# Scatters of gathered rows with at most two under way, in a fused attention and mixture-of-experts kernel

## The chip, the cores and the metric

The kernel runs on 1 core of one Trainium2 chip, as one program with one launch. The metric is the device time of an execution in microseconds (us); the median of several executions is compared. Lower is better.

## What is computed

Two layers on x of 8 batches x 512 tokens x 256 channels. The first is cross-attention with 16 heads of 16 channels, the second a mixture of 8 experts of which each token uses 2.

```python
x = x + xattn(layernorm(x), ctx)      # 16 heads, softmax(q k^T / 4) v, then wo
t = layernorm(x)
probs = softmax((t @ Wg + bg) / 5.0)
vals, idx = top_k(probs, 2)
gates = mask(vals, idx) / (sum + 1e-9)
h = gelu(t @ W1[e] + b1[e])           # hidden size 512, each expert e
y = sum_e gates[e] * (h @ W2[e] + b2[e])
x = x + y
```

Everything is float32; products are made of two or three float32r products where they must be exact.

## The kernel before, in words

The program is written by hand for each engine, with semaphores, and there is no scheduler. Each engine runs its own list in order.

**Attention.** Eight bodies, one for each batch (`body(i)` on every engine), each of four units of four heads. A unit has eight steps of 1.7 to 2 us. In a step TensorE makes two score products (L1542 for the maximum that VectorE takes at L1113, L1555 for the exponentials that ScalarE takes at L1041) and the products with the values (L1568). Between the steps stand the small units of work of earlier and later batches, which the tables `PREP`, `POST`, `LATE` and `LAST_POST` place at a group and step: "OP0" to "OP3" (the output projection, L1619, taken by VectorE at L1166), "V0" and "V1" (the values of the next batch, L1609), "MT" (the transposed maxima, L1577), "XG0" and "XG1" (the transposes of the normalised rows `xg`, L1586), "LG" (the gate logits, L1629) and "PX" (positions of the chosen rows).

**Routing and scatters.** For each batch b, `ln2(b)` on POOL (L791 to L807) writes the normalised rows into `xg` (128 partitions x 4 tiles x 265 floats: 256 channels, 8 gates, the token's number). VectorE adds the gates and computes in `route_rows` which row of `xs_dram` (the experts' regions in device memory) each token's copy goes to. POOL's `scatter_tile(k, t)` (L813) then sends one tile of 128 rows with an indirect DMA: 8 of them for a batch, for choice k = 0, 1 and tile t = 0 to 3. Each adds 16 to the one semaphore `scattered` when it has landed. There are 64 in all:

- batches 0 to 4 in bodies 2 to 6 (`scatter(i - 2, ...)`, L818), each held back until step 5 and later steps of unit 1 by a wait on `st_full`;
- batch 5 in body 7, without that pacing;
- batch 6 in the tail, one before each of the tiles 1 to 8, and batch 7 before each of the tiles 25 to 32 (L930 to L937).

`ln2(b + 1)` follows the eight scatters of the batch on POOL and waits at L796 until all of them have landed, since it writes `xg` again. Behind it on POOL stand `add_bo`, `place_v` (L871, which waits for TensorE's L1568 of the body) and `low_staged` (L830). SP waits for `xg_done` in `load_w2` (L572), and in body 7 for the scatters of batches 0 to 5 before its first `load_rows`. VectorE waits for those of batches 0 to 6 in `apply_last`.

**Tail.** 71 tiles of 128 rows: SP loads a tile from `xs_dram` (L625), TensorE makes hidden and output products (L1716, L1734), VectorE scales the result into `y_sb` (L1467), and POOL's `add_out(j)` (L922) adds it into `out` with an indirect DMA, after reading from a table for how many earlier ones it has to wait. POOL's list is `add_out` and, between them, the scatters.

All DMAs of POOL go through one queue (q0 in the profile), those of SP through another (q1).

Of the kernel before, what the change touches and what calls it, by code (L numbers as in the profile page):

```python
# [14 lines left out]
P = 128  # L15
B, S, D = 8, 512, 256
H, DH = 16, 16
NT = S // P
# [185 lines left out]
def build(nc, x, ctx_kv, wqT, bq, wkT, bk, wvT, bv, woT, bo, wg, bg, w1, b1, w2, b2, out):  # L204
    with ExitStack() as stack:
# [185 lines left out]
        kv_in, qk_weights_in = sem("kv_in"), sem("qk_weights_in")  # L391
        ones_set, ident_set, bq_scaled = sem("ones_set"), sem("ident_set"), sem("bq_scaled")
        warm_set = sem("warm_set")
# [26 lines left out]
        chosen_done, rows_done, token_chain = sem("chosen_done"), sem("rows_done"), sem("token_chain")  # L420
        scattered, padded = sem("scattered"), sem("padded")
        pad_rows_done, tab_done = sem("pad_rows_done"), sem("tab_done")
# [31 lines left out]
        def w2_hi_free(eng, e):  # L454

            if e < 2:
                eng.wait_ge(st_full, NP * G)
            elif e < 6:
                eng.wait_ge(pv_done, NT * (G - 1) + (2 if e < 4 else 1))
            else:  # L460
                eng.wait_ge(st_full, NP * (G - 1))

        def stage_no(i, n):
# [6 lines left out]
        def _(sp):  # L470
# [156 lines left out]
            def body(i):  # L627
# [54 lines left out]
                if not more:  # L682
                    sp.wait_ge(tab_done, 1)
                    sp.wait_ge(scattered, 16 * TOPK * NT * EARLY_B)
                    for j in range(EARLY_XS + 1):
                        load_rows(j)
# [58 lines left out]
            for j in range(AHEAD, TILES):  # L745
                if j == TAIL_STORE:
                    store_out(B - 1)
                if j == TAIL_PAD:
                    pad_regions()
                if j == TILES1:  # L750
                    sp.wait_ge(tab_done, 2)
                    sp.wait_ge(scattered, 16 * TOPK * NT * B)
                    sp.wait_ge(padded, 16 * (E + 1))
                load_rows(j)
# [3 lines left out]
        def _(pool):  # L758
            nc.gpsimd.memset(ident[:], 0.0).then_inc(pool_chain, 1)
            pool.wait_ge(pool_chain, 1)  # L760
            nc.gpsimd.affine_select(out=ident[:], in_=ident[:], compare_op=ALU.not_equal, fill=1.0, base=0,
                                    pattern=[[-1, P]], channel_multiplier=1).then_inc(ident_set, 1)
            nc.gpsimd.memset(mhalf[:], -0.5).then_inc(pool_chain, 1)
            nc.gpsimd.memset(oT[0:2, 0, :], 1.0).then_inc(ones_set, 1)
            nc.gpsimd.memset(pad[:], 0.0).then_inc(ones_set, 1)
            for g in range(NG):
                nc.gpsimd.memset(kq[g][:, 1].bitcast(F32), 0.0).then_inc(ones_set, 1)
            pool.wait_ge(pool_chain, 2)
            pool.wait_ge(stats_done, 1)
            nc.gpsimd.tensor_tensor(rstd[:], veps[:], mhalf[:], ALU.pow).then_inc(rstd_done, 1)  # L770
            nc.gpsimd.memset(v_aug[:], 0.0).then_inc(pool_chain, 1)
            pool.wait_ge(pool_chain, 3)
            nc.gpsimd.memset(v_aug[:, :, :, DH:DH + 1], 1.0).then_inc(pool_chain, 1)
            pool.wait_ge(pool_chain, 4)
            nc.gpsimd.memset(before[:], 1.0).then_inc(pool_const, 1)
# [15 lines left out]
            def ln2(b):  # L791
                pool.wait_ge(ln2_stats, b + 1)
                nc.gpsimd.tensor_tensor(rstd2[:], veps2[:], mhalf[:], ALU.pow).then_inc(rstd2_done, 1)
                if b > 0:
                    pool.wait_ge(scattered, 16 * TOPK * NT * b)
                    pool.wait_ge(full["XG1"], b)  # L796
                    pool.wait_ge(token_chain, 2 * b)
                else:
                    pool.wait_ge(pool_const, 11)
# [13 lines left out]

            def scatter_tile(k, t):
                pool.indirect_dma_start(out=xs_dram, out_offset=bass.IndirectOffsetOnAxis(ap=rows[:, k, t:t + 1], axis=0),  # L815
                                        in_=xg[:, t, :], in_offset=None).then_inc(scattered, 16)

            def scatter(b, paced=None):  # L818
                rows_ready(b)
                for k in range(TOPK):  # L820
                    for t in range(NT):
                        if paced is not None:

                            pool.wait_ge(st_full, paced + NT * k + t)
                        scatter_tile(k, t)

# [100 lines left out]
            for j in range(TILES):  # L927
                if j == TAIL_POW:
                    ln2(B - 1)
                if j == TAIL_SCATTER_BEFORE:  # L930
                    rows_ready(B - 2)
                if TAIL_SCATTER_BEFORE <= j < TAIL_SCATTER_BEFORE + TOPK * NT:
                    scatter_tile(*divmod(j - TAIL_SCATTER_BEFORE, NT))
                if j == TAIL_SCATTER:
                    rows_ready(B - 1)
                if TAIL_SCATTER <= j < TAIL_SCATTER + TOPK * NT:
                    scatter_tile(*divmod(j - TAIL_SCATTER, NT))  # L937
                if j == TILES1:
                    pool.wait_ge(out_done, 16 * B)
                    pool.wait_ge(need_done, 2)  # L940
                add_out(j)
# [164 lines left out]
        def _(dve):  # L1106
# [82 lines left out]
            def apply_last(b, half):  # L1189
                dve.wait_ge(rstd2_done, b + 1)  # L1190
                dve.wait_ge(full["XG1"], b)
                dve.wait_ge(scattered, 16 * TOPK * NT * b)
                for t in (2 * half, 2 * half + 1):
# [318 lines left out]
        def _(pe):  # L1512
# [155 lines left out]
            for n in range(WARM):  # L1668
                nc.tensor.matmul(ring[2][:, 1, :], xgT[:, 0, 0:P], xgT[:, 0, :], start=True, stop=True)
            pe.wait_ge(ident_set, 1)  # L1670
            for name in PROLOGUE:
# [125 lines left out]
```

## Time and profile before

| | us |
|---|---|
| median of 3 executions | 808.66 |
| their range | 805.75 to 810.44 |
| profiled execution, its own time | 804.46 |
| profiled execution, its span | 802.4 |
| TensorE busy in the span | 755.2 |
| VectorE busy | 612.2 |
| ScalarE busy | 455.1 |
| POOL busy | 393.9 |
| mean granted TensorE clock | 0.992 |

The span is the time between the first and the last instruction of the profile; the execution's own time holds 2.06 us around it. Times in the rows are from the span's start. "Idle before" in brackets is how long the engine stood still before the instruction and what released it; "issue" is time in which it waited for nothing that the profile shows, "remote" a release that the profile can't name. TensorE's ends are modelled.

### The profile page before, as it was taken

The page shows a single profiled execution, that of the slowest core. Times are in us where ns is not written, and L with a number is a line of the kernel's source. Part 1 is how long each engine was busy: PE and PEld are TensorE (multiplying, and loading weights), DVE is VectorE, ACT ScalarE, POOL GpSimd, SP SyncE. Part 2 cuts the span into 40 slices and gives each one's busy share as a digit, 9 for nine tenths or more (in the row PEclk, how much of TensorE's full clock was granted, in tenths as well). Part 3 has the DMA queues.
Part 4 walks back from the last instruction along what each step waited for, and adds up shares of the span by engine and source line. Part 5 has one row for each costly group of instructions (what it writes and reads, how often), then busy time and mean ns, then how long its engine had stood idle before and what let it go on. Part 6 is the DMA issues. An engine that isn't in the chain of part 4 may idle for free.

```text
span 802.4 us, 16337 instructions
## 1 busy us (share of the span) xinstructions
PE 755.2 (94%) x4672; PEld 451.9 (56%) x4672; DVE 612.2 (76%) x1126; ACT 455.1 (57%) x663; POOL 393.9 (49%) x357
## 2 busy tenths in 40 slices
PE   9999999999999999999999898869999999999994
PEld 4443344444444444444444333349989888999994
DVE  6787778798697787788788787667777887776773
ACT  2066676776766766766676674854345443444441
POOL 6506143547637728728725613306553564444443
PEclk9999999999999999999999999999999999999998
DMA  7665857657666767757658467666454465454441
GB/s 226 208 179 176 228 165 226 209 179 250 206 188 239 213 198 234 190 188 250 186 174 268 149 178 260 257 241 161 89 101 80 79 145 93 74 84 70 72 69 12
DMA packets 90660, 136.24 MB, mean 170 GB/s; under 512 B 15456, under 2 KB 49216, under 8 KB 90192
## 3 DMA queue, kind: packets, MB, share of 16 engines
q1 hardware_dynamic: 76592, 117.33, 48.0%
q0 software_dynamic: 13296, 17.09, 12.1%
q8 instruction: 43, 0.70, 0.4%
q10 hardware_dynamic: 688, 0.79, 0.3%
q14 instruction: 41, 0.34, 0.1%
HBM read 71.25 MB, written 64.04 MB: 169 GB/s over the span
## 4 chain that ended last, share of the span: by engine, by line
PE 71%; DMA 7%; DVE 7%; ACT 6%; issue 5%; SPq 2%; POOL 1%; POOLq 0%; DVEq 0%; another core or an unknown queue 0%
PE ps_pv L1568 13%; PE ring L1555 10%; PE ring L1734 9%; PE ring L1716 8%; PE ring L1542 7%; PE ps_x L1599 7%; ACT probs L1041 4%; PE ps_x L1619 4%; DMA out<-y_sb,xs 3%; PE ps_x L1609 3%; PE ring L1725 3%; DVE negm L1113 2%; PE ps_x L1629 2%; DMA den<-oT 2%; PE ps_pv L1707 1%
## 5 line engine op out<-in xcount | busy, mean ns | idle before, releaser
L1113 DVE TENSOR_REDUCE negm<-ring 128x2 f32<-128x1024 f32 x256 | 310.2, 1222 | 73.0 <-PE ring L1542 65.0
L1041 ACT ACTIVATE probs<-ring 128x1024 f32<-128x1024 f32 x256 | 260.0, 1024 | 91.7 <-PE ring L1555 79.4
L922 POOL DMA_INDIRECT out<-y_sb,xs x71 | 110.2, 1553 | 152.3 <-DMA out<-y_sb,xs 73.6
L1568 PE MATMUL ps_pv<-probs,v_aug 128*32 128x512 f32 x1024 | 136.8, 606 | 4.0 <-ACT probs L1041 3.9
L1555 PE MATMUL ring<-kq 64*128 64x512 f32 x512 | 125.4, 491 | 7.5 <-DVE negm L1113 7.3
L1542 PE MATMUL ring<-kq 64*128 64x512 f32 x512 | 105.9, 412 | 10.6 <-ACT probs L1041 5.4
L1555 PEld LDWEIGHTS ring<-kq 64*128 64x128 f32 x512 | 47.4, 183 | 108.5 <-issue 72.4
L1074 ACT CAST xsT_hi<-ps_pv 128x256 fp32r<-128x256 f32 x70 | 26.1, 373 | 133.8 <-PE ps_pv L1707 122.9
L1734 PE MATMUL ring<-w_hi,hT_hi 128*128 x284 | 85.3, 300 | 0.1
L815 POOL DMA_INDIRECT xs_dram<-xg,rows x64 | 63.3, 988 | 39.9 <-issue 15.9
L1734 PE MATMUL ring<-w_lo,hT_hi 128*128 x284 | 80.0, 282 | 0.0
L1734 PE MATMUL ring<-w_hi,hT_lo 128*128 x284 | 79.5, 280 | 0.0
L1455 DVE TENSOR_TENSOR h_pre<-ring,b_sb 128x512 f32<-128x512 f32 x71 | 48.9, 690 | 20.8 <-PE ring L1716 19.0
L1542 PEld LDWEIGHTS ring<-kq 64*128 64x128 f32 x512 | 48.7, 186 | 26.7 <-issue 10.8
L1716 PE MATMUL ring<-w_hi,xsT_hi 128*128 x142 | 58.8, 414 | 4.4 <-DVE xsT_lo L1443 3.2
L855 POOL CAST qk_hi<-qk 128x512 fp32r<-128x512 f32 x28 | 17.1, 611 | 86.0 <-ACT qk L977 54.3
L871 POOL TENSOR_TENSOR v_aug<-v_flat,bv_sb 128x256 f32<-128x256 f32 x32 | 23.7, 756 | 71.0 <-PE ps_pv L1568 61.0
L1716 PE MATMUL ring<-w_hi,xsT_lo 128*128 x142 | 56.4, 397 | 0.0
L1716 PE MATMUL ring<-w_lo,xsT_hi 128*128 x142 | 56.2, 396 | 0.0
L1734 PEld LDWEIGHTS ring<-w_hi,hT_hi 128*128 128x128 f32 x284 | 53.6, 189 | 0.2 <-issue 0.2
L1734 PEld LDWEIGHTS ring<-w_lo,hT_hi 128*128 128x128 f32 x284 | 53.6, 189 | 0.0
L1734 PEld LDWEIGHTS ring<-w_hi,hT_lo 128*128 128x128 f32 x284 | 53.5, 188 | 0.0
(197 smaller groups left out, 1223.4 us busy)
## 6 DMA issues: line engine op xcount, KB each, us to landing
kq<-k_dram SPq DMA_DIRECT2D x64, 192.0 KB
kq<-q_dram SPq DMA_DIRECT2D x64, 192.0 KB
xs<-xs_dram SPq DMA_DIRECT2D x71, 132.5 KB
k_dram<-qk_hi SPq DMA_DIRECT2D x32, 256.0 KB
q_dram<-qk_hi SPq DMA_DIRECT2D x32, 256.0 KB, 2.8
o_dram<-oT SPq DMA_DIRECT2D x32, 256.0 KB
w_dram<-w_sb SPq DMA_DIRECT2D x12, 512.0 KB
w_hi<-w_dram SPq DMA_DIRECT2D x12, 512.0 KB, 7.4
```

The lines of the kernel that those rows point to most:

```text
L815: pool.indirect_dma_start(out=xs_dram, out_offset=bass.IndirectOffsetOnAxis(ap=rows[:, k, t:t + 1], axis=0), in_=xg[:, t, :], in_offset=No ...
L922: pool.indirect_dma_start(out=out, out_offset=bass.IndirectOffsetOnAxis(ap=xs[j % AHEAD][:, TOKEN:TOKEN + 1].bitcast(I32), axis=0), in_=y_ ...
L1041: nc.scalar.activation(probs[kt][:, 2 * jp:2 * jp + 2, :], ring[PLACE["ST", u, p] % RINGS][:], ACT.Exp).then_inc(exp_done, 1)
L1113: nc.vector.tensor_reduce(negm[:, v % 2, :, jp, kt], ring[PLACE["MX", v, p] % RINGS][:], AX.X, ALU.max, negate=True).then_inc(max_free, 1)
L1455: v.tensor_tensor(h_pre[:, j % 2, :], ps_h[j % 2], b1_sb[:, bass.ds(e, 1), :].rearrange("p o h -> p (o h)"), ALU.add).then_inc(f_h_out, 1)
L1542: mm = nc.tensor.matmul(ps[:, h, :], kq[g][lo:lo + HALF, 1, jp, kt * P:(kt + 1) * P], kq[g][lo:lo + HALF, 0, jp, :], start=True, stop=True)
L1555: mm = nc.tensor.matmul(ps[:, h, :], kq[g][lo:lo + HALF, 0, jp, kt * P:(kt + 1) * P], kq[g][lo:lo + HALF, 1, jp, :], start=True, stop=True)
L1568: mm = nc.tensor.matmul(ps_pv[2 * DH * j:2 * DH * (j + 1), :], v_aug[:, kt, HPG * g + j, :], probs[kt][:, j, :], start=(kt == 0), stop=(kt ...
L1599: mm = nc.tensor.matmul(ps[:, half], w[:, c, f * P:(f + 1) * P], act_t[:, c, half], start=(c == 0), stop=(c == DC - 1))
L1619: mm = nc.tensor.matmul(ps[:, (t % 2) * D:(t % 2 + 1) * D], numT[:, c, t * P:(t + 1) * P], wo_sb[:, c, :], start=(c == 0), stop=(c == DC - 1))
L1716: mm = nc.tensor.matmul(ps_h[j % 2], x[:, j % 2, c, :], w[:, bass.ds(e, 1), c, :].rearrange("p o h -> p (o h)"), start=(n == 0), stop=(n = ...
L1734: mm = nc.tensor.matmul(ps_y[j % 2][:, 0:D], h[:, j % 2, c, :], w[:, bass.ds(e, 1), c, :].rearrange("p o d -> p (o d)"), start=(n == 0), s ...
```

## The change

`scattered` becomes two semaphores, used in turn by the number n of the scatter (0 to 63). From the third on, a scatter waits on POOL until all scatters of its own semaphore before it have landed: scatter n waits for scatter n - 2. Whoever waited for the first b batches now waits for both semaphores. To make room for the second one, `ident_set` goes away: the identity's `affine_select` counts in `pool_chain`, whose later thresholds go up by one, and TensorE waits there for 2. No instruction moves to another place on any engine.

```diff
-        ones_set, ident_set, bq_scaled = sem("ones_set"), sem("ident_set"), sem("bq_scaled")
+        ones_set, bq_scaled = sem("ones_set"), sem("bq_scaled")
...
-        scattered, padded = sem("scattered"), sem("padded")
+        scattered, padded = [sem(f"scattered{n}") for n in range(2)], sem("padded")
...
+        def wait_scattered(eng, b):
+
+            for n in range(2):
+                eng.wait_ge(scattered[n], 16 * TOPK * NT * b // 2)
...
-                    sp.wait_ge(scattered, 16 * TOPK * NT * EARLY_B)
+                    wait_scattered(sp, EARLY_B)
...
-                    sp.wait_ge(scattered, 16 * TOPK * NT * B)
+                    wait_scattered(sp, B)
...
-                                    pattern=[[-1, P]], channel_multiplier=1).then_inc(ident_set, 1)
+                                    pattern=[[-1, P]], channel_multiplier=1).then_inc(pool_chain, 1)
...
-            pool.wait_ge(pool_chain, 2)
+            pool.wait_ge(pool_chain, 3)
...
-                    pool.wait_ge(scattered, 16 * TOPK * NT * b)
+                    wait_scattered(pool, b)
...
-            def scatter_tile(k, t):
+            def scatter_tile(b, k, t):
+
+                n = NT * (TOPK * b + k) + t
+                if n >= 2:
+                    pool.wait_ge(scattered[n % 2], 16 * (n // 2))
                 pool.indirect_dma_start(out=xs_dram, out_offset=bass.IndirectOffsetOnAxis(ap=rows[:, k, t:t + 1], axis=0),
-                                        in_=xg[:, t, :], in_offset=None).then_inc(scattered, 16)
+                                        in_=xg[:, t, :], in_offset=None).then_inc(scattered[n % 2], 16)
...
-                    scatter_tile(*divmod(j - TAIL_SCATTER_BEFORE, NT))
+                    scatter_tile(B - 2, *divmod(j - TAIL_SCATTER_BEFORE, NT))
...
-                    scatter_tile(*divmod(j - TAIL_SCATTER, NT))
+                    scatter_tile(B - 1, *divmod(j - TAIL_SCATTER, NT))
...
-                dve.wait_ge(scattered, 16 * TOPK * NT * b)
+                wait_scattered(dve, b)
...
-            pe.wait_ge(ident_set, 1)
+
+            pe.wait_ge(pool_chain, 2)
```

## Rows read from the trace of the kernel before

**Rows 1.** The page: busy time by engine, and the chain that ended last
```profile
PE 755.2 (94%) x4672; PEld 451.9 (56%) x4672; DVE 612.2 (76%) x1126; ACT 455.1 (57%) x663; POOL 393.9 (49%) x357
...
PE 71%; DMA 7%; DVE 7%; ACT 6%; issue 5%; SPq 2%; POOL 1%; POOLq 0%; DVEq 0%; another core or an unknown queue 0%
```

**Rows 2.** POOL's instructions in order, batch 0's scatters: start, length, [idle before]
```profile
189.04 1.27 POOL L815 DMA_INDIRECT xs_dram<-xg,rows  x1 [0.19 <-issue]
...
190.61 0.97 POOL L815 DMA_INDIRECT xs_dram<-xg,rows  x1 [0.30 <-issue]
...
195.67 0.96 POOL L815 DMA_INDIRECT xs_dram<-xg,rows  x1 [0.30 <-issue]
...
199.31 0.96 POOL L815 DMA_INDIRECT xs_dram<-xg,rows  x1 [0.30 <-issue]
...
203.89 0.20 POOL L800 CAST xg<-token 128x4 int32<-128x4 f32 x1 [1.40 <-DMA xs_dram<-xg,rows]
```

**Rows 3.** The same view, the last scatter of batch 1 and its follower
```profile
261.42 0.96 POOL L815 DMA_INDIRECT xs_dram<-xg,rows  x1 [0.30 <-issue]
...
267.29 0.19 POOL L800 CAST xg<-token 128x4 int32<-128x4 f32 x1 [2.09 <-DMA xs_dram<-xg,rows]
```

**Rows 4.** Stretches 190 to 202 us: busy times, granted clock, DMA share, GB/s
```profile
193.00:196.00 3.00, 3.00 (x19) 1.28 (x13) 3.00 (x4) 2.35 (x4) 2.25 (x3) 1.00 0.30 103
...
196.00:199.00 3.00, 2.06 (x16) 0.54 (x14) 1.58 (x4) 1.20 (x2) 1.58 (x2) 1.00 0.95 256
```

**Rows 5.** POOL after the batch of body 2, and SP's queue in that body
```profile
224.41 0.74 POOL L871 TENSOR_TENSOR v_aug<-v_flat,bv_sb 128x256 f32<-128x256 f32 x1 [7.58 <-PE ps_pv L1568]
...
215.99 0.40 SPq L572 DMA_DIRECT2D x_all<-in_L_ffn_W  x1
...
225.15 0.54 SPq L513 DMA_DIRECT2D kq<-mT  x1
```

**Rows 6.** POOL in body 7: the batch without pacing and ln2 behind it
```profile
487.77 1.11 POOL L815 DMA_INDIRECT xs_dram<-xg,rows  x1 [14.49 <-DVEq L1281]
...
496.79 0.96 POOL L815 DMA_INDIRECT xs_dram<-xg,rows  x1 [0.30 <-issue]
...
505.59 1.04 POOL L793 TENSOR_TENSOR rstd<-veps,mhalf 128x4 f32<-128x4 f32 x1 [7.85 <-DVE veps L1187]
...
506.80 4.95 POOL L804 TENSOR_SCALAR xg<-x_all,mv,rstd 128x256 f32<-128x256 f32 x4
```

**Rows 7.** TensorE in body 7: the transposes of xg
```profile
512.13 0.66 PE L1586 MATMUL ps_x<-ident,xg 128*128 128x128 f32 x4
```

**Rows 8.** Stretches of body 7, columns as in rows 4
```profile
487.00:495.00 8.00, 6.64 (x33) 2.68 (x33) 6.67 (x8) 3.48 (x4) 5.70 (x6) 0.79 1.00 356
...
501.00:504.00 3.00, 2.56 (x18) 1.35 (x18) 3.00 (x5) 1.37 (x2) 0.00 (x0) 1.00 0.00 0
```

**Rows 9.** POOL in the tail: a scatter and the last but one before it
```profile
565.19 0.98 POOL L815 DMA_INDIRECT xs_dram<-xg,rows  x1 [0.31 <-issue]
...
571.51 0.98 POOL L815 DMA_INDIRECT xs_dram<-xg,rows  x1 [0.30 <-issue]
```

**Rows 10.** The chain that ended last, in order of time: start, us, what
```profile
573.12 5.72 DMA out<-y_sb,xs
...
792.31 2.70 DMA out<-y_sb,xs
```

**Rows 11.** TensorE: MT and V0 in body 1, then in body 2
```profile
133.06 0.28 PE L1577 MATMUL ps_x<-ident,negm 128*16 128x128 f32 x1
...
137.37 0.92 PE L1609 MATMUL ps_x<-wv_sb,kvT 128*128 128x256 f32 x3
...
193.80 0.28 PE L1577 MATMUL ps_x<-ident,negm 128*16 128x128 f32 x1
...
199.31 0.92 PE L1609 MATMUL ps_x<-wv_sb,kvT 128*128 128x256 f32 x3
```

**Rows 12.** VectorE in body 7, just after the sixth scatter
```profile
497.83 0.42 DVE L1166 TENSOR_TENSOR x_all<-x_all,ps_x 128x256 f32<-128x256 f32 x1 [2.46 <-remote]
```

More of the change, by code:

```diff
@@ L771, in _ @@
             nc.gpsimd.memset(v_aug[:], 0.0).then_inc(pool_chain, 1)
-            pool.wait_ge(pool_chain, 3)
+            pool.wait_ge(pool_chain, 4)
             nc.gpsimd.memset(v_aug[:, :, :, DH:DH + 1], 1.0).then_inc(pool_chain, 1)
-            pool.wait_ge(pool_chain, 4)
+            pool.wait_ge(pool_chain, 5)
             nc.gpsimd.memset(before[:], 1.0).then_inc(pool_const, 1)
@@ L824, in scatter @@
                             pool.wait_ge(st_full, paced + NT * k + t)
-                        scatter_tile(k, t)
+                        scatter_tile(b, k, t)
             def low_staged(i, n):
```

## The prediction

> **What bounds the kernel now.** I read the page first: TensorE is busy for 755.2 us of 802.4 (94%), and the chain that ended last is TensorE's for 71%, while POOL has 1% of it [rows 1]. So work on POOL costs time only where somebody waits for it. The scatters are 64 POOL instructions of about 1 us, and the question is how long one needs to land, for which of the 64 the new wait is not met yet, and who stands behind POOL then.
>
> POOL's own list shows the first batch [rows 2]. Its first scatter starts at 189.04, the second at 190.61, the sixth at 195.67, the eighth at 199.31: a first step of 1.57 us, then 1.265 us each ((195.67 - 190.61) / 4), a little more at the last two, which the pacing holds. The follower at L800 waits for the landing and starts at 203.89, that is 4.58 us after the eighth scatter began. In batch 1 the same distance is 267.29 - 261.42 = 5.87 us [rows 3]. I call this distance L: from the start of a scatter to the start of an instruction that waits for its landing. Both are taken where SP's transfers crowd in: the share of the DMA engines is 0.95 in 196 to 199 us. Three microseconds before it is only 0.30, at 103 GB/s [rows 4]; one scatter moves 128 x 265 x 4 = 135,680 bytes, which at 1.265 us each is 107 GB/s. So the scatters land as fast as they are issued there, and nothing piles up. For a quiet queue the nearest row is the add_out near the end: 2.70 us from its start to its landing [rows 10].
>
> **The change part by part.** With the new wait scatter n can't start before n - 2 has landed. Two can be under way, so a batch of eight becomes four pairs: if L is the same for all, the last has landed 1.57 + 4 L after the first began. The wait binds where L is over twice the step, 2.53 us.
>
> *L, from both sides.* It can't be under the 0.96 us in which POOL itself works on the instruction [rows 2]; the highest row is 5.87. I take 2.70 for scatters that meet an idle queue (nearest row, add_out) and 5.87 for those that meet a full one. By the Trainium skill, page "DMA: Bandwidth & Descriptors", section "Anatomy of one DMA — SWDGE (gpsimd) path", a DMA from this queue costs about 2.0 us plus its bytes at 436 GB/s, most of it the receipt of the write; an estimate by it is 2.31 us, with the 0.96 before it 3.27, and by it the batch in body 7 would have landed after 14.7 us and delay nobody. The rows say up to 5.87, and by that a batch takes 25.05 us; I reckon with the rows.
>
> *Bodies 2 to 6* (40 scatters). Now the follower of a batch starts 14.85 us after its first scatter (203.89 - 189.04). With L = 2.70 the last scatter could start after 3 x 2.70 + 1.57 = 9.67 us, and it starts at 10.27 already now, so nothing moves. With 5.87 throughout the follower comes 10.2 us later. What covers it: POOL stands idle for 7.58 us before its L871 at 224.41, waiting for TensorE [rows 5]; SP issues the load at L572, which waits for xg, at 215.99, and its next urgent one, the maxima of L513, at 225.15 [rows 5]. ln2 now ends at about 209 us (203.89 + 0.20 + 4.84 for the four tiles, the same length as in body 7 [rows 6]), 7 us before SP's turn; even 10.2 us late it would hold SP for 3.2 us, inside the stretch before 225.15. Expected delay 0 to 1 us on POOL, on the end 0. Both ends are 0 as well.
>
> *Body 7* (8 scatters). This is the tight place. The scatters begin at 487.77 without pacing. ln2 starts at 505.59, held by VectorE's statistics and not by them, and its next instruction, which does wait for them, can start at 506.63. It then makes xg until 511.75 (506.80 + 4.95) [rows 6], and TensorE takes its transposes at 512.13 [rows 7], with only 0.38 us between. So the scatters may take 506.63 - 487.77 = 18.86 us, and the point from which they delay TensorE is L = (18.86 - 1.57) / 4 = 4.32 us. In 487 to 495 us the DMA engines are full (share 1.00), in 501 to 504 they stand idle (0.00) [rows 8]. I take 5.87 for the first pair and 2.70 for the three others: 1.57 + 5.87 + 3 x 2.70 = 15.54 us, landed at 503.3, 3.3 us early. Cost 0; the ends are 0 and, with 5.87 for all, 25.05 - 18.86 = 6.2 us. SP's wait for the six batches stands later still and needs nothing earlier.
>
> *Tail* (16 scatters). Here a scatter and the last but one are at least one add_out and a tile apart, as 565.19 and 571.51, 6.32 us [rows 9]. The longest landing that the chain shows there is an add_out's of 5.72 us [rows 10], the scatters' own highest is 5.87. So the wait is met, by 0.45 us at the worst. This matters, since POOL is on the chain in this stretch. Value 0.
>
> *The waits themselves.* Scatters in bodies 2 to 6 carry a wait (`st_full`), those in the tail carry none, and both start 0.30 us after the instruction before [rows 2, 9]. A wait that is met costs nothing visible. I take 0; the upper end is another 0.30 us for each of the about six tail scatters that stand where POOL is on the chain, 1.8 us. In the bodies 8 x 0.30 us would vanish in the 7.58 us of idle time.
>
> *The identity's semaphore.* POOL's list keeps its order, count 2 of `pool_chain` is reached by the same instruction as before, and the memset that counts 3 ran before the same wait. Cost 0.
>
> **Sum.** 804.46 (the profiled execution, span 802.4) + 0 = 804.5. The median of the three is 4.2 us above that execution, so for the median the sum is 808.66 + 0, and I say 808.8 for the few waits that may show. A change of 0.5% (4.04 us) is about what a measurement of this kernel can tell from none; the three executions differ by 4.7 us.
>
> **The rivals.**
>
> *Faster: a standstill that comes with the bursts.* From MT to V0 TensorE needs 137.37 - 133.06 = 4.31 us in body 1, which has no scatters, and 199.31 - 193.80 = 5.51 in body 2 [rows 11], with the same work. The 1.20 us fall just behind the sixth scatter (195.67). In body 7, where neither the step nor SP's list is the same, VectorE stands for 2.46 us before 497.83 with no named release [rows 12], again behind the sixth scatter. If this comes from transfers that pile up, fewer under way could end it: 5 x 1.20 + 2.46 = 8.5 us, 800.3. Against it: in body 2 the step and the traffic before the standstill say that no more than about two are under way already (DMA share 0.30), so the wait hardly changes the moment at which it comes. By the Trainium skill, the same page, section "Queues, rings and completion order", each DMA engine takes turns between the queues by packets, so that a shorter POOL queue would leave SP's transfers more turns. By that rule the trace agrees in so far as the standstill of body 2 comes where both queues are in use [rows 4]. The rival's chance is 0.16.
>
> *Slower: body 7's batch lands late.* If L stays at 5.87 for all four pairs (SP's loads in front [rows 8]), ln2 waits, xg comes 6.2 us late, TensorE stands at XG0 and with it everything to the tail: 815.0. It decides from L = 4.32 on; at 4.58 it is 1.0 us. For it: 4.58 and 5.87 are what POOL really waited elsewhere. Against it: the queues are empty after 501 us. Chance 0.11 for over half of it.
>
> *The change does nothing at all.* With L under 2.53 no wait ever binds. That is 808.7, not to be told from the forecast by time, only by POOL's rows; it is counted with it.
>
> **How the numbers follow.** Forecast, with the case of no binding wait, 0.73: 808.8, own range 805.5 to 812 by the scatter of the executions. Faster rival 0.16 (800.3, in part 804), slower rival 0.11 (815.0, in part 812). The range takes in most of the faster case and half of the slower: 801.0 to 813.5. Faster by over 0.5%: 0.17. Slower by over 0.5%: 0.12. Within: 0.71.
>
> **What would show it.** Right: in bodies 2 to 6 POOL's scatters still start 1.3 to 1.6 us apart for the first six, with short waits for a landing at most at the last two, ln2 within 1 us of where it was; in body 7 a wait of 3 to 5 us before the third scatter, all eight landed before 506; no wait for a scatter in the tail; MT to V0 still 5.5 us in body 2. Wrong: POOL waiting for landings at every pair, XG0 in body 7 later than 512 by more than a microsecond with ln2 as its releaser, waits for landings before scatters in the tail (then add_out and VectorE's L1467 are late behind them), or MT to V0 back at 4.3 us.

## The result: 1.5% slower, and the profile after

The changed kernel takes 820.3 us (median of 6 executions, 814.49 to 824.88), the kernel before beside it 809.82 (805.75 to 810.84): ratio 1.0154, 95% interval 1.0116 to 1.0192. The forecast of no difference was wrong, and 820.3 lies outside the range of 801.0 to 813.5. The profiled execution took 816.67 us, with a span of 814.6 us; before it was 804.46 and 802.4.

The page of the changed kernel: busy time by engine (to read beside [rows 1]), and the group of all scatters (line, engine, what | busy, mean ns | idle before, by releaser).
```profile
PE 759.5 (93%) x4672; PEld 452.1 (56%) x4672; DVE 611.1 (75%) x1126; ACT 456.4 (56%) x663; POOL 393.7 (48%) x357
...
L824 POOL DMA_INDIRECT xs_dram<-xg,rows x64 | 63.0, 985 | 73.7 <-DMA xs_dram<-xg,rows 29.3
```
TensorE is busy for 4.3 us more with the same 4672 instructions, which points to its clock (mean granted 0.981, before 0.992); the rest of the 12.2 us of span is idle time. POOL now waits 29.3 us for landings in front of scatters. Who pays for them is not POOL.

POOL in the changed kernel, batch 0 and what follows it (start, length, what, [idle before <-releaser]), which answers to [rows 2]:
```profile
189.06 1.27 POOL L824 DMA_INDIRECT xs_dram<-xg,rows  x1 [0.19 <-issue]
190.63 0.97 POOL L824 DMA_INDIRECT xs_dram<-xg,rows  x1 [0.30 <-issue]
193.68 0.96 POOL L824 DMA_INDIRECT xs_dram<-xg,rows  x1 [2.08 <-DMA xs_dram<-xg,rows]
...
196.91 0.96 POOL L824 DMA_INDIRECT xs_dram<-xg,rows  x1 [1.01 <-DMA xs_dram<-xg,rows]
199.91 0.96 POOL L824 DMA_INDIRECT xs_dram<-xg,rows  x1 [2.03 <-DMA xs_dram<-xg,rows]
202.56 0.96 POOL L824 DMA_INDIRECT xs_dram<-xg,rows  x1 [1.70 <-PE ring L1564]
204.88 0.96 POOL L824 DMA_INDIRECT xs_dram<-xg,rows  x1 [1.36 <-PE ring L1564]
205.86 1.06 POOL L798 TENSOR_TENSOR rstd<-veps,mhalf 128x4 f32<-128x4 f32 x1
211.89 0.20 POOL L805 CAST xg<-token 128x4 int32<-128x4 f32 x1 [4.97 <-issue]
```
The third scatter starts 4.62 us after the first, the last 15.8 us after it where it was 10.3. Its follower at L805 comes another 7.01 us later, at 211.89 instead of 203.89: ln2 is 8.0 us late.

SP in that moment: its load of the next expert's w1 (512 KB), the largest transfer near the last scatter. Two of 256 KB go out just before it, at 203.44 and 204.42.
```profile
205.06 0.45 SPq L480 DMA_DIRECT2D w_sb<-in_L_ffn_W  x1
```

TensorE in the kernel before, body 2: MT, XG0 and the next MT. (MT comes four times in a body. "Unit 1" is from here on the stretch from the MT of [rows 11], at 193.80 in body 2, to the next at 210.27, and "unit 2" the one behind it, with XG0 in it.)
```profile
210.27 0.28 PE L1577 MATMUL ps_x<-ident,negm 128*16 128x128 f32 x1
...
214.19 0.66 PE L1586 MATMUL ps_x<-ident,xg 128*128 128x128 f32 x4
...
224.13 0.28 PE L1577 MATMUL ps_x<-ident,negm 128*16 128x128 f32 x1
```
The same of the changed kernel, and XG0 of bodies 3 to 6:
```profile
209.10 0.28 PE L1586 MATMUL ps_x<-ident,negm 128*16 128x128 f32 x1
...
217.05 1.08 PE L1595 MATMUL ps_x<-ident,xg 128*128 128x128 f32 x4 [3.96 <-POOL xg L809]
...
229.24 0.28 PE L1586 MATMUL ps_x<-ident,negm 128*16 128x128 f32 x1
...
284.47 0.84 PE L1595 MATMUL ps_x<-ident,xg 128*128 128x128 f32 x4 [3.71 <-POOL xg L809]
...
349.35 0.88 PE L1595 MATMUL ps_x<-ident,xg 128*128 128x128 f32 x4 [2.90 <-POOL xg L809]
...
412.81 0.63 PE L1595 MATMUL ps_x<-ident,xg 128*128 128x128 f32 x4 [1.44 <-POOL xg L809]
...
474.36 0.63 PE L1595 MATMUL ps_x<-ident,xg 128*128 128x128 f32 x4 [1.25 <-POOL xg L809]
```
Before, xg was ready at 204.07 + 4.84 = 208.9 (L804 starts right behind the follower) and read at 214.19: TensorE's margin was 5.3 us (4.0 to 5.5 in the other four bodies), and a delay of 8.0 us breaks it. That alone makes a wait of 2.7 us; TensorE also comes 1.2 us earlier than before (its MT is at 209.10, not 210.27), and so waits 3.9. Over the five bodies it waits 3.96, 3.71, 2.90, 1.44 and 1.25 us, 13.3 in all, and unit 2 grows from 13.86 to 20.14 us in body 2, over the five bodies from 69.1 to 86.8: 17.7 us. The other 4.4 stand in bodies 2 to 4, where the granted clock is 0.50 for 6.8, 3.4 and 3.4 us from about the end of the wait on. Windows of the changed kernel (us, PE, PEld, DVE, ACT, POOL busy, granted clock, DMA share, GB/s):
```profile
216.00:223.00 7.00, 5.95 (x24) 2.63 (x24) 1.23 (x1) 2.23 (x4) 7.00 (x7) 0.53 0.92 314
```
and of the kernel before:
```profile
216.00:223.00 7.00, 6.89 (x52) 3.71 (x44) 5.40 (x6) 4.27 (x5) 0.83 (x1) 1.00 1.00 334
```
Half a microsecond before the end of the wait of 3.96 us the granted clock falls to its lower level, 1.2 GHz, and stays there for 6.8 us, and 24 matmuls start where 52 did.

Something was won as well. MT and V0 of body 2, changed kernel, beside [rows 11]:
```profile
193.83 0.28 PE L1586 MATMUL ps_x<-ident,negm 128*16 128x128 f32 x1
...
198.13 1.99 PE L1618 MATMUL ps_x<-wv_sb,kvT 128*128 128x256 f32 x8
```
4.30 us, not 5.51: the standstill behind the sixth scatter is gone. Unit 1 takes 15.27 or 15.28 us in every body, where it took 16.45 to 16.88: 6.8 us less over five bodies. The first scatter of body 7 thus starts 17.7 - 6.8 + 0.8 (the other units) = 11.7 us late, at 499.43.

Body 7 in the changed kernel, POOL, to read beside [rows 6]:
```profile
499.43 1.11 POOL L824 DMA_INDIRECT xs_dram<-xg,rows  x1 [14.49 <-DVEq L1290]
...
506.57 0.96 POOL L824 DMA_INDIRECT xs_dram<-xg,rows  x1 [4.75 <-DMA xs_dram<-xg,rows]
...
515.18 0.96 POOL L824 DMA_INDIRECT xs_dram<-xg,rows  x1 [0.70 <-DMA xs_dram<-xg,rows]
...
520.30 0.19 POOL L805 CAST xg<-token 128x4 int32<-128x4 f32 x1 [2.92 <-issue]
```
and TensorE, its MT and XG0, beside [rows 7]:
```profile
513.79 0.28 PE L1586 MATMUL ps_x<-ident,negm 128*16 128x128 f32 x1
...
525.48 1.08 PE L1595 MATMUL ps_x<-ident,xg 128*128 128x128 f32 x4 [4.20 <-POOL xg L809]
```
Eight scatters and the follower take 20.87 us against the 18.86 that I had allowed, and TensorE waits 4.20 us. The stretch before it is 2.6 us shorter (16.51 us from MT to MT, before 19.08), so the first add_out is 13.7 us late and the last 12.1. The tail between them is 1.6 us shorter than before (252.6 us for 254.2). In the twenty profiled executions of this document the tail lasts 251.8 to 258.8 us, so nothing is read from that difference.

POOL in the tail of the changed kernel:
```profile
578.45 0.98 POOL L824 DMA_INDIRECT xs_dram<-xg,rows  x1 [0.30 <-issue]
...
584.76 0.98 POOL L824 DMA_INDIRECT xs_dram<-xg,rows  x1 [0.30 <-issue]
```
No wait for a landing there, and 0.30 us before each of the 16 as in [rows 9].

### The profile page after: what moved, and what is told of

The parts are those of the page before. It is cut to its first block and busy times, and to the rows that moved or that the text cites. A ratio compares the mean times of both kernels' runs of the same rounds, so it can differ in the third digit from the quotient of the medians.

```text
span 814.6 us, 16384 instructions
## 1 busy us (share of the span) xinstructions
PE 759.5 (93%) x4672; PEld 452.1 (56%) x4672; DVE 611.1 (75%) x1126; ACT 456.4 (56%) x663; POOL 393.7 (48%) x357
## 3 DMA queue, kind: packets, MB, share of 16 engines
q0 software_dynamic: 13296, 17.09, 12.1%
## 5 line engine op out<-in xcount | busy, mean ns | idle before, releaser
L1577 PE MATMUL ps_pv<-probs,v_aug 128*32 128x512 f32 x1024 | 140.7, 622 | 3.0 <-ACT probs L1050 2.7
L824 POOL DMA_INDIRECT xs_dram<-xg,rows x64 | 63.0, 985 | 73.7 <-DMA xs_dram<-xg,rows 29.3
L1457 DVE TENSOR_TENSOR hT_lo<-ring,hT_hi 128x512 fp32r<-128x512 f32 x71 | 48.8, 688 | 4.7 <-ACT hT_hi L1089 1.1
```

The costliest lines, as they stand in the source:

```text
L1457: v.tensor_tensor(hT_lo[:, j % 2], ps_ht[j % 2].rearrange("p (c t) -> p c t", t=P), hT_hi[:, j % 2].bitcast(F32), ALU.subtract).then_inc(f ...
L1577: mm = nc.tensor.matmul(ps_pv[2 * DH * j:2 * DH * (j + 1), :], v_aug[:, kt, HPG * g + j, :], probs[kt][:, j, :], start=(kt == 0), stop=(kt ...
```

## The experiments

They ran in five sessions, each beside executions of the kernel before on the same chip; its median was 805.9 and 806.0 us in the first two and 795.7, 795.5 and 798.0 in the others. That difference became a finding; across sessions only ratios are compared. The chip had number 12, 5, 0, 0 and 5, so under number 5 the kernel before took 806.0 us once and 798.0 another time.

### Which waits cost: none, bodies 2 to 6, body 7, the tail

These are the changed kernel, with the wait in `scatter_tile` under another condition. Shown is the one for body 7; for bodies 2 to 6 it is `2 <= n < 40`, for the tail `n >= 48`. The first kernel has no wait at all, only the two semaphores.
```
-                if n >= 2:
+                if 40 <= n < 48:
                     pool.wait_ge(scattered[n % 2], 16 * (n // 2))
```


> The change without its waits before the scatters: two semaphores in turn, nobody held back. Theory A (the time is lost because the batch's last scatter lands late, ln2 waits for it, and TensorE stands at XG0): as the kernel before, 809.8 us, no wait at XG0, and MT to V0 again 5.5 us in body 2. Theory B (each wait costs by itself, or the bookkeeping of two semaphores): over 812 us even so.

> Waits only before the scatters of bodies 2 to 6 (38 of the 62). Theory A: these bodies lose 17.7 us at XG0 (waits of 1.3 to 4.0 us and a slower clock behind them) and win back 6.7 us at the standstill, so about 820.5 us. Theory B, waits of equal price: 38/62 of the loss of 10.5 us, 816 us.

> Waits only before the eight scatters of body 7. Theory A: 2.6 us won at the standstill and about 4 lost at XG0, 811 us. Theory B: 8/62 of 10.5 us, 811 us. The trace tells: under A the standstill before 497.8 is gone and XG0 comes late.

> Waits only before the 16 scatters of the tail. Theory A: met at once, 809.8 us. Theory B: 16/62 of 10.5 us, 812.5 us, or more, since POOL is on the chain there.

Measured: no waits 805.73 us, ratio 0.9985 (0.9955 to 1.0014); bodies 2 to 6 811.51, 1.0070 (1.0036 to 1.0103); body 7 806.70, 1.0006 (0.9981 to 1.0030); tail 805.99, 1.0005 (0.9971 to 1.0039). So the two semaphores, the identity's count and the tail's waits show no cost, as forecast, and bodies 2 to 6 cost. But they cost about half of what theory A forecast (820.5 beside 809.8, a ratio of 1.013), and the 1.0070 is what the rival of equal prices gave (816, 1.008): these four times alone don't decide between the two. That rival falls later, with kernels that keep many waits and lose nothing by them.

The profiled execution with the waits of bodies 2 to 6 has the changed kernel's picture: unit 1 at 15.27 us, unit 2 at 19.87, 18.30, 19.75, 14.76 and 14.39. It took 819.95 us, 8.4 more than its kernel's median, so it shows where the time goes, and not how much a typical execution loses. In body 7 alone the slow side and the fast side cancel. TensorE there, and the window behind its XG0 (columns as above):
```profile
501.16 0.28 PE L1586 MATMUL ps_x<-ident,negm 128*16 128x128 f32 x1
...
510.27 0.87 PE L1595 MATMUL ps_x<-ident,xg 128*128 128x128 f32 x4 [1.62 <-POOL xg L809]
```
```profile
510.00:524.00 14.00, 13.73 (x60) 6.87 (x60) 4.94 (x16) 8.00 (x11) 0.33 (x2) 0.52 0.87 321
```
The stretch to this MT shrank from 19.08 to 16.51 us, and XG0 waits 1.62 us, with the clock at 0.52 in 510 to 524. (With no waits in body 7 that stretch varies among these four kernels: 17.66 us with no waits at all, 17.73 with those of bodies 2 to 6, 19.73 with those of the tail.) The batch and its follower took 18.25 us, less than the 18.86 that I had allowed; TensorE waits all the same, because without the standstill it comes sooner. The parts sum to about 0.8%, the whole was 1.5% in its session: when body 7's batch follows late bodies, XG0 waits 4.20 us instead of 1.62. That is at most a part of the gap, and the rest stays open.

### Is it TensorE's margin at XG0? The transposes later, with a control

The transposes move two steps back, and the two halves of the gate logits become one piece of work.
```
-        (3, 3): "XG0", (3, 4): "XG1", (3, 5): "LG0", (3, 7): "LG1"}
+        (3, 5): "XG0", (3, 6): "XG1", (3, 7): "LG"}
```


> The change, and XG0, XG1 and LG of bodies 2 to 6 two steps (about 3.5 us) later, at steps 5, 6 and 7 of the last unit. Theory A (TensorE waits at XG0 for the late batch, and its clock falls behind that wait): waits of 4.0, 3.7, 2.9, 1.4 and 1.3 us shrink to 0.5 us at most, the clock stays up, the 6.7 us won at the standstill remain, so 14 us less than the change, about 806 in its scale of 820 and at or below the kernel before. Theory B (waits cost wherever they stand): within 2 us of the change.

> The kernel before with XG0, XG1 and LG of bodies 2 to 6 two steps later and nothing else: the control of e1. Both theories: as before within 1 us, since TensorE does the same work and nothing waits for LG early.

Measured: the changed kernel with it 812.83 us, 1.0080 (1.0043 to 1.0116); the kernel before with it 813.58, 1.0090 (1.0055 to 1.0126). The move itself costs 0.9%, where none was expected, so it is no remedy, but beside this control the change costs nothing, with all its 62 waits in place. XG0 of body 2, with the waits and the late transposes:
```profile
222.07 0.66 PE L1595 MATMUL ps_x<-ident,xg 128*128 128x128 f32 x4
```
No wait, although the last scatter starts at 210.65; of bodies 3 to 6 one has a wait, of 0.29 us. So with the waits at XG0 of these bodies gone, the loss is gone too, or the main part of it: the 6 us of standstills should then have shown as a gain, and didn't. Body 7, which the move leaves as it was, still waits 2.42 us; unit 2 took 2.5 us more in sum than in the control, and one other unit grew to 18.08 us, with 6.8 us at half clock at its start.

### Keeping the gain without the loss: fewer waits, or a pace

First the changed kernel without waits for the last two scatters of a batch, then the kernel before with a later pace (each scatter of bodies 2 to 6 is held by a softmax tile two steps later) and no wait for a landing.
```
-                if n >= 2:
+                if n >= 2 and n % 8 < 6:
```
```
-SCATTER = 5
+SCATTER = 7
```


> The change without the waits before the last two scatters of each batch. Theory A: those two start up to 2.5 us earlier and ln2 comes 2 to 3 us earlier in bodies 2 to 6, so XG0 waits 1 us or less in place of up to 4: 8 to 10 us less than the change. The standstill stays away. Theory B: 16 of 62 waits fewer, 3 us less.

> The kernel before with one semaphore and no wait for a landing, but the pacing of the scatters two steps later (SCATTER 7): from the fifth on one scatter for each step, some 1.8 us apart where it was 1.27. Theory C1 (the standstill behind the sixth scatter comes from six in a row at 1.27 us): the first MT interval of bodies 2 to 6 falls from 16.5 to 15.3 us, the last scatter is 3 us later and ln2 within the 5 us that XG0 leaves: 6 us faster. Theory C2 (it comes from the number of scatters, however spaced): 16.5 us stays, time as before.

Measured: first six 800.09 us, 0.9923 (0.9888 to 0.9959); paced 801.74, 0.9951 (0.9915 to 0.9987). Both beat the kernel before, in a session where it took 805.98 and the control above, with the same scatters, still has unit 1 at 16.22 to 16.77 us. In both unit 1 is 15.27 us and unit 2 13.87 (13.67 in body 6). The first of them keeps 46 of the 62 waits. The last scatter of batch 0 and its follower, first six:
```profile
202.46 0.96 POOL L824 DMA_INDIRECT xs_dram<-xg,rows  x1 [0.30 <-issue]
...
205.46 0.20 POOL L805 CAST xg<-token 128x4 int32<-128x4 f32 x1 [0.94 <-DMA xs_dram<-xg,rows]
```
and paced:
```profile
202.53 0.96 POOL L815 DMA_INDIRECT xs_dram<-xg,rows  x1 [0.71 <-PE ring L1555]
...
205.66 0.20 POOL L800 CAST xg<-token 128x4 int32<-128x4 f32 x1 [1.09 <-DMA xs_dram<-xg,rows]
```
They start 3.2 us later than in the kernel before, and the follower only 1.6 to 1.8 us later, inside TensorE's 5.3. Two waits fewer move the last scatter by 2.4 us, and the follower by 6.4. In body 7 the first of them still waits, 2.42 us at XG0.

### Three under way, and one pause only

```
-        scattered, padded = [sem(f"scattered{n}") for n in range(2)], sem("padded")
+        scattered, padded = [sem(f"scattered{n}") for n in range(3)], sem("padded")
...
-                if n >= 2:
-                    pool.wait_ge(scattered[n % 2], 16 * (n // 2))
+                if n >= 3:
+                    pool.wait_ge(scattered[n % 3], 16 * (n // 3))
```
and, in another kernel, `if n % 8 in (2, 3):` in the place of `if n >= 2:`.

> The changed kernel with three semaphores in turn instead of two: each scatter waits for the last but two. Theory (margin and standstill): the change lost its time because the last scatter of a batch started 5.6 us later (204.88 for 199.31), past the 5.3 us by which TensorE reads xg late at XG0, and won back about 1.3 us a body because the standstill behind six scatters in a row went. With three under way only the sixth, the seventh and the eighth wait at all, by one to two us: last scatter of batch 0 at 200.5 to 202.5, rows of batch 1's ln2 copied (L805) at 204 to 206, no wait of TensorE at XG0, unit 2 of a body 13.9 us. If the standstill hangs on how many scatters are under way, unit 1 is 15.3 us and the time 799 to 803; if it hangs only on six issues at 1.27 us one behind the other, it is gone too where the sixth is held. Rival (any wait for a landing costs TensorE its clock, whatever the margin): half clock in the bodies as in the changed kernel and a time of 810 or more.

> The changed kernel with the wait only before the third and fourth scatter of a batch, so that one pause of about 1.8 us is left and the other six scatters follow at 1.27 us (the seventh and eighth by the work's own pace). Theory: last scatter of batch 0 at 200 to 201, ln2's copy at 204, unit 2 of a body 13.9 us, no wait at XG0. The standstill: if it needs six scatters at 1.27 us in an unbroken row, the row is now third to eighth, and either it comes behind the eighth or, with the pace of the seventh, it is gone; if it hangs on the bytes that stand in the queue, it comes back behind the sixth (unit 1 16.5 us). Time 799 to 803 without it, 804 to 807 with it. Rival (each wait for a landing costs by itself): half of the changed kernel's loss, 810 to 813.

Measured: 798.3 us, 1.0013 (0.9993 to 1.0033), and 797.8, 1.0014 (0.9991 to 1.0036). In microseconds both are about a microsecond below the 799 to 803 that were expected, with unit 1 at 15.27, unit 2 at 13.86, and no wait at XG0 in bodies 2 to 6, so the rivals that any wait for a landing costs, or each the same, are out. But the kernel before took 795.74 us beside them: there was nothing to win. In body 7 of the first, TensorE stands for 1.04 us and then, at XG0, for 0.92; behind that its granted clock is at 0.51 for 14 us, though it is busy all the time (columns as above):
```profile
506.00:520.00 14.00, 14.00 (x60) 6.92 (x60) 5.10 (x17) 8.18 (x11) 0.02 (x1) 0.51 0.80 293
```
The question about the standstill was not answered by them; it was asked again below.

### The slow landing: SP's w1 load a step later

```
-                if i < B - 2:
+                if i == 0:
                     load_w1(i)
-                if i == 0:
                     load_w1(E - 2)
                 if more:
                     put_max(i + 1, 0)
                     load_stack(i + 1, 2)
+                    if 0 < i < B - 2:
+                        load_w1(i)
```


> The changed kernel, but SP's load of the next expert's w1 in bodies 1 to 5 (L480, at 205.06 in body 2, 0.2 us behind the last scatter's start) is issued one step later, behind the next V's keys and queries (about 212). Theory (the last scatter is slow because it stands behind this load): from its start to ln2's copy falls from 7.0, 6.4, 5.8 and 5.6 us in bodies 2 to 5 to 4.0 to 4.4, body 6, which has no such load, stays at 4.3; TensorE's wait at XG0 falls by the same 1.4 to 2.7 us; time 3 to 8 us below the changed kernel. Rival (the load is innocent, the landing is slow for another reason, such as the stores and fetches before it): 5.6 to 7.0 us as before and no change of the time.

> The control of the run before: the same later w1 load in the kernel before the change. There the last scatter starts 5.7 us ahead of that load and lands ahead of it, so both theories expect no difference beyond 0.3% (804 to 808 us); a gain or a loss here is what moving the load does by itself, and is to be taken off the other run's.

Measured: the changed kernel with it 805.76 us, 1.0118 (1.0070 to 1.0167); the kernel before with it 797.09, 1.0005 (0.9979 to 1.0031). From the last scatter's start to the follower it now takes 3.99, 4.60, 4.72 and 4.89 us in bodies 2 to 5, not 7.01, 6.44, 5.77 and 5.59. The waits at XG0 of bodies 2 to 6 are 0.94, 1.60, 0.57, 1.81 and 1.23 us, 6.2 in all instead of 13.3, though the one in body 5 is longer than the 1.44 it had. The forecast of 4.0 to 4.4 was a little short. And the control showed unit 1 at 15.27 us in the kernel before, with none of its edits near the scatters.

### Is the standstill always there? Four kernels in one session

The kernel before, the changed kernel, the latter with the late w1 load, and the paced kernel, each unchanged from above.

> The kernel before, unchanged, to have its trace on the same chip as the next three. Theory (the standstill belongs to the chip's own speed at taking packets, not to the kernel alone): where unit 1 of a body lasts 16.4 to 16.9 us the time is about 806, where it lasts 15.3 us it is about 797. Rival (the standstill went in the last four runs through their edits): unit 1 lasts 16.4 us or more in every body of this run, whatever its time.

> The changed kernel, on the same chip. Waits of TensorE at XG0 in bodies 2 to 6 of 1.2 to 4.0 us, unit 2 of a body 15 to 20 us, unit 1 15.3 us. Theory: the loss against the kernel before is the growth of unit 2 (about 17 us) and of body 7 (about 3) less what the standstills took: 1.2 to 1.8 per cent where the kernel before has them, 2.0 to 2.8 per cent where it has not. Rival (the gain never came from the standstill): the same 1.5 per cent on every chip.

> The changed kernel with SP's w1 load of bodies 1 to 5 behind the next V's keys and queries, on the same chip as the changed kernel. Theory: the last scatter's start to ln2's copy is 4.0 us instead of 5.6 to 7.0, TensorE's wait at XG0 is 1 to 2.5 us shorter, and the time is 6 to 11 us below the changed kernel's: about half of the loss was this load. Rival (the loss is the waits alone, the landing does not matter): the time is that of the changed kernel within 3 us.

> The kernel before with its scatters paced by the softmax's tiles two steps later, no wait for a landing. Theory: where the kernel before has the standstill this is 0.5 to 1.2 per cent faster (unit 1 at 15.3 us), where it has not it is the same within 0.3 per cent. Rival (pacing gains by something else): 0.5 per cent faster or more on either.

Measured, beside 795.46 us: the kernel before under its own label 797.09, 1.0027 (1.0010 to 1.0045); changed 814.10, 1.0258 (1.0185 to 1.0330); with the late load 807.55, 1.0140 (1.0104 to 1.0175); paced 795.77, 0.9997 (0.9973 to 1.0022). The first of these, the same kernel twice, shows that 0.3% can come from nothing.

The kernel before beside them, the seventh and eighth scatter on POOL, and TensorE's MT, V0 and MT:
```profile
197.37 0.96 POOL L815 DMA_INDIRECT xs_dram<-xg,rows  x1 [0.30 <-issue]
198.65 0.96 POOL L815 DMA_INDIRECT xs_dram<-xg,rows  x1 [0.32 <-PE ring L1555]
```
```profile
194.23 0.28 PE L1577 MATMUL ps_x<-ident,negm 128*16 128x128 f32 x1
...
198.53 1.99 PE L1609 MATMUL ps_x<-wv_sb,kvT 128*128 128x256 f32 x8
...
209.50 0.28 PE L1577 MATMUL ps_x<-ident,negm 128*16 128x128 f32 x1
```
MT to V0 is 4.30 us and unit 1 15.27 with eight scatters in an unbroken row of 1.27 us: no standstill, in any body. The rival, that it was the edits, is out. (The seventh scatter stood 2.38 us behind the sixth in the first trace, and stands 1.27 behind it here: what held it there was the standstill, by way of the softmax tile that it waits for.) Without a standstill the change has nothing to gain, and costs 2.6% instead of 1.5; the paced kernel gains nothing either, as expected. How the 2.6% come about is not shown by the profiled execution. Unit 2 sums to 75.9 us there, 6.9 more than in the kernel before beside it and not the 17 expected; the first add_out is 9.2 us late, and 4.9 us more fall in the tail, where no wait stands. In four profiled executions with the waits of bodies 2 to 6, unit 2 takes 17.7, 17.9, 6.9 and (further below) 11.2 us more than the 69.1 of the kernel before. The late load took 6.5 us from the changed kernel's time. Its profiled execution didn't say why, with waits at XG0 of about the same sum, so both ran again.

> The changed kernel again. Theory: in bodies where SP's w1 load is issued within half a microsecond of the last scatter's start, ln2's copy comes 5.8 to 7 us after that start and TensorE waits 3 to 4 us at XG0, behind which its granted clock is at 1.2 GHz for some microseconds; where the load comes over 1.2 us later, 4.2 to 5.6 us and waits under 1.5 us.

> The changed kernel with the w1 load of bodies 1 to 5 a step later, again. Theory: from the last scatter's start to the copy 4.0 to 5.4 us in every body, no wait at XG0 above 2.2 us, the time 4 to 9 us below the changed kernel's. Rival (the gain is elsewhere, or chance): the sum of the five waits at XG0 is within 2 us of the changed kernel's, and the time too.

Measured, beside 797.98 us: changed 813.48, 1.0199 (1.0158 to 1.0239); late load 807.24, 1.0126 (1.0088 to 1.0164). Again about 6 us apart. Body 5 of the changed kernel, first SP's load:
```profile
394.64 0.45 SPq L480 DMA_DIRECT2D w_sb<-in_L_ffn_W  x1
```
then POOL's last scatter and its follower:
```profile
394.41 0.96 POOL L824 DMA_INDIRECT xs_dram<-xg,rows  x1 [1.44 <-DMA xs_dram<-xg,rows]
...
400.68 0.19 POOL L805 CAST xg<-token 128x4 int32<-128x4 f32 x1 [4.23 <-issue]
```
and TensorE's XG0:
```profile
405.85 1.09 PE L1595 MATMUL ps_x<-ident,xg 128*128 128x128 f32 x4 [3.07 <-POOL xg L809]
```
The same body with the late load, POOL:
```profile
389.40 0.96 POOL L825 DMA_INDIRECT xs_dram<-xg,rows  x1 [0.30 <-issue]
...
394.37 0.19 POOL L806 CAST xg<-token 128x4 int32<-128x4 f32 x1 [2.93 <-issue]
```
and XG0:
```profile
399.54 0.63 PE L1596 MATMUL ps_x<-ident,xg 128*128 128x128 f32 x4 [0.81 <-POOL xg L810]
```
6.27 us and a wait of 3.07, against 4.97 and 0.81. In the three profiled executions of the changed kernel, the six last scatters with the w1 load issued within half a microsecond of their start landed 5.8 to 7.0 us later (7.01, 6.44, 5.77; 6.33; 6.16, 6.27); the other six, where the load came 0.7 us or more behind, took 4.2 to 5.6. With the late load, in three executions, all twelve took 4.0 to 5.3. The kernels with waits in bodies 2 to 6 alone and with the late transposes say the same: seven scatters with the load that close took 5.5 to 6.8 us, an eighth with the load 2.4 us behind took 5.3. The waits at XG0 of bodies 2 to 5 sum to 9.0 us here and 4.3 with the late load. In the pair before they were 5.3 and 6.0, so that this load delays the landing is shown body by body, but single executions scatter as much as the effect, and that it accounts for all of the 6 us is not shown.

## Why the prediction was wrong

**Bodies 2 to 6: the failed step.** "Expected delay 0 to 1 us on POOL, on the end 0. Both ends are 0 as well." I took POOL's idle time before L871 and SP's turn at L572 for the cover and did not ask who else reads xg. XG0 does, 5.3 us after it is made in body 2. My own upper end, 10.2 us late, passes that margin by 4.9 us; the measured 8.0 us lie inside it. What the runs showed in the place of "both ends are 0": waits of 3.96, 3.71, 2.90, 1.44 and 1.25 us at XG0, and unit 2 longer by 17.7 us in that execution. So the bound on a whole batch held and the cover was wrong, and the end of the range with it. In body 7 I had looked at XG0 [rows 7], and in the others not.

**L, mis-sized.** For a quiet queue I took 2.70 us, an add_out's landing. Scatters 1 and 3 are 4.62 us apart, and even paced scatters need 2.8 to 3.2 us to the follower. The last one takes 7.01 us, over my 5.87; the waits had moved it beside SP's w1 load, and with that load later it took 3.99. The Trainium skill, page "DMA: Bandwidth & Descriptors", section "Anatomy of one DMA — SWDGE (gpsimd) path", puts a DMA from this queue at about 2.0 us plus its bytes at 436 GB/s, an estimate of 2.31 us here and 3.27 with POOL's 0.96 before it; the paced kernel comes near that (3.13, 2.94, 2.93, 3.24, 2.87), the full queue does not.

**Body 7.** Forecast 0 with an upper end of 6.2 us; the slower rival named it. Here the margin was broken too, by 20.87 us against 18.86. My 5.87 for the first pair was short: the third scatter came 7.14 us after the first. And the 18.86 was taken from an execution with the standstill: in the one without, the follower starts 497.61 - 481.35 = 16.26 us after the first scatter, 2.6 less. So with the waits of body 7 alone the batch took 18.25 us and TensorE still waited 1.62. What the standstill gave back paid for that wait and for the clock behind it: alone it shows no cost (1.0006).

**Tail, waits that are met, identity's semaphore.** Right: 0 within what was measured (tail 1.0005, up to 1.0039), 0.30 us before each as before, and 0.9985 without waits.

**The faster rival.** The gain that it named was there: 6.8 us in bodies 2 to 6 and 2.6 in body 7 (8.5 were estimated). That transfers which pile up were the cause is not shown. I gave it 0.16 by arguing that the wait would hardly change the moments of the first six scatters; it did. The third scatter already starts 1.8 us later than before, the sixth 4.2. What the standstill is stays open: it came behind six scatters in a row in some sessions, and in others not with eight.

**The forecast's chances.** Slower by over 0.5% was put at 0.12, with body 7 as its only place; its real place was in five bodies. That its 815.0 lies near the measured 820.3 is luck.

## What to carry to other kernels

When a change makes something late, list every reader of what it produces and take the smallest margin, above all on the engine that is the bound; an idle producer is no cover. A throttle on a queue has two prices, the round trip for each pair, and what the last transfer meets at its new time; leaving out the last two waits turned 1.5% slower into 0.8% faster, in sessions that had the standstill. A margin is to be taken anew when the change also makes its reader earlier. And a gain that comes from a standstill has to be looked for in several sessions, since with none to remove only the price stays.

## What the runs showed of the hardware

- A standstill of about 1.2 us on TensorE (and of 2.5 us on VectorE in body 7) behind the sixth scatter in a row at 1.27 us, in sessions where the kernel before took 806 to 810 us, and absent with the same kernel in one where it took 795.5. In body 2 ScalarE's next L1041 (197.81 us, idle for 2.22) and POOL's seventh scatter (198.05, idle for 1.42) were late with it. In the slower sessions it was gone when waits held the third, fifth and sixth scatter (steps of 1.5 to 4.2 us there) and when all stood 1.65 to 2.6 us apart. One pause alone was tried only where the standstill was absent anyway. Whether it belongs to the chip was not settled.
- Last scatters with a 512 KB load issued on SP's queue within half a microsecond of their start were about 1.2 us slower to land, by the mean, than those with the load 0.7 to 2.4 us behind (thirteen of 5.5 to 7.0 us against seven of 4.2 to 5.6).
- With TensorE's wait of 3.96 us at XG0 its granted clock was 0.53 over 216 to 223 us, near the lower level of 1.2 GHz. After the waits of 1.44 and 1.25 us there was no such stretch. All five waits and their aftermath took 17.7 us in that execution, of which the idle time itself is 13.3.
- A short wait can cost clock too: in body 7 waits of 1.62 us (body 7 alone) and of 1.04 and 0.92 us two microseconds apart (three under way) were followed by 14 us at 0.52 and 0.51, with TensorE busy for 13.73 and 14.00 of them.
